# Packed key/value projection, input split moved into the last query tiles, last denominators summed apart from matmuls

## The reference

```
qkv = x @ Wqkv.T + b          # 16 query heads of 32, one key head and one value head of 32
P   = softmax(causal(q k.T / sqrt(32)));  ctx = P v;  a = ctx @ out_w.T + out_b
x1  = layernorm(x + a)        # no gain or bias
s   = x1 @ router_w.T         # 8 experts, the best 2, softmax of their 2 scores
y   = sum over the two experts of weight * (silu(x1 w1[e]) * (x1 w3[e])) w2[e]   # bf16
out = layernorm(x1 + y)
```

## Time and profile before

| | |
|---|---|
| time, median of 3 runs | 1130.98 us (1130.84 to 1131.72) |
| the profiled execution | 1128.94 us, span 1126.9 us |
| PE busy | 1083.4 us, 96% |
| DVE, ACT, POOL busy | 883.7, 718.4, 194.6 us |
| mean granted PE clock | 0.992 |
| scores L1170, values L1192 on PE | 327.3 and 286.7 us |
| exponentials L652 on ACT | 525.4 us |
| adds L829 on DVE | 403.4 and 64.0 us |

### The profile page before, as it was taken

One profiled execution on the slowest core, in us unless ns is written; L12 is line 12 of the kernel. 1 busy time (PEld: TensorE's weight loads), 2 busy tenths in 40 slices (PEclk: granted clock), 3 DMA queues, 4 the chain that ended last, 5 costly groups with the idle time before them and its releaser, 6 DMA issues.

```text
span 1126.9 us, 18411 instructions
## 1 busy us (share of the span) xinstructions
PE 1083.4 (96%) x6096; PEld 524.6 (47%) x6120; DVE 883.7 (78%) x1105; ACT 718.4 (64%) x852; POOL 194.6 (17%) x161
## 2 busy tenths in 40 slices
PE   8999999999999999999999999999999999999976
PEld 6365435643337433335634643474333654333442
DVE  4566899679976699987677679966998667898956
ACT  6744785478864498885445457644888437888821
POOL 3520332013110020111032013301211201211000
PEclk9899999999999999999999999999999999999999
DMA  4976401442001622001263253025400152200000
GB/s 141 210 115 145 119 1 39 103 122 39 1 2 47 141 76 38 1 1 40 64 143 98 58 130 75 3 59 130 113 1 1 39 122 67 39 1 2 1 2 38
DMA packets 40336, 72.31 MB, mean 64 GB/s; under 512 B 13968, under 2 KB 14992, under 8 KB 40208
## 3 DMA queue, kind: packets, MB, share of 16 engines
q1 hardware_dynamic: 24624, 56.64, 19.0%
q0 software_dynamic: 13584, 11.54, 7.0%
q10 hardware_dynamic: 2000, 2.51, 0.7%
HBM read 25.58 MB, written 8.39 MB: 30 GB/s over the span
## 4 chain that ended last, share of the span: by engine, by line
PE 80%; DVE 10%; issue 5%; POOL 2%; ACT 2%; DMA 1%; SPq 1%; DVEq 0%; ACTq 0%; POOLq 0%
PE sc L1170 21%; PE bank L1192 19%; PE sc L1032 10%; PE sc L1310 9%; PE bank L1032 7%; DVE psum_k L829 5%; PE sc L1210 3%; PE sc L1325 2%; PE bank L1210 2%; PE sc L1258 1%; POOL prob L517 1%; PE bank L1318 1%; DVE stats L905 1%; PE bank L1325 1%; DVE res L902 1%
## 5 line engine op out<-in xcount | busy, mean ns | idle before, releaser
L652 ACT ACTIVATE prob<-sc 128x1024 f32<-128x1024 f32 x544 | 525.4, 1025 | 130.8 <-PE sc L1170 130.7
L829 DVE TENSOR_TENSOR psum_k<-psum_k,prob 128x2048 f32<-128x2048 f32 x170 | 403.4, 2373 | 4.7
L1170 PE MATMUL sc<-q_st,k_st 128*128 128x512 f32 x1088 | 327.3, 423 | 9.4 <-DVE rden L878 3.8
L1170 PEld LDWEIGHTS sc<-q_st,k_st 128*128 128x128 f32 x1088 | 184.5, 189 | 250.6 <-ACT prob L652 177.3
L1192 PE MATMUL bank<-prob,v_sb 128*32 128x512 f32 x2176 | 286.7, 604 | 1.2 <-POOL prob L517 1.2
L517 POOL TENSOR_SCALAR_AFFINE_SELECT prob<-prob 128x1024 f32<-128x1024 f32 x64 | 113.2, 1817 | 530.7 <-ACT prob L652 530.7
L1310 PE MATMUL sc<-prob,w_sb 128*128 128x512 bf16 x488 | 116.9, 379 | 2.1 <-issue 1.3
L1192 PEld LDWEIGHTS bank<-prob,v_sb 128*32 128x32 f32 x2176 | 44.4, 108 | 105.5 <-issue 87.4
L682 ACT ACTIVATE prob<-sc 128x512 f32<-128x512 f32 x64 | 38.0, 594 | 73.0 <-PE sc L1310 72.7
L829 DVE TENSOR_TENSOR psum_k<-prob 128x2048 f32<-128x2048 f32 x28 | 64.0, 2287 | 20.7 <-POOL prob L517 16.2
L1032 PE MATMUL bank<-q_st,wq_hi 128*128 128x512 f32 x240 | 80.1, 398 | 0.0
(11 more groups left out here) (155 smaller groups left out, 1017.8 us busy)
## 6 DMA issues: line engine op xcount, KB each, us to landing
q_st<-q_hi SPq DMA_DIRECT2D x120, 128.0 KB, 2.4
q_st<-q_lo SPq DMA_DIRECT2D x120, 128.0 KB, 2.4
res<-in_x SPq DMA_DIRECT2D x8, 1024.0 KB, 5.2
res<-ob_sb POOLq DMA_DIRECT2D x8, 1024.0 KB, 8.6
out_x<-res SPq DMA_DIRECT2D x32, 256.0 KB, 2.0
res<-in_xT SPq DMA_DIRECT2D x7, 1024.0 KB, 4.9
w_sb<-in_w POOLq DMA_DIRECT2D x8, 256.0 KB, 8.6
prob<-in_wqkvT ACTq DMA_DIRECT2D x4, 288.0 KB, 6.3
```

Of the source, the lines that this page charges most:

```text
L652: nc.scalar.activation(prob[t % NP][:, half * HW:(half + 1) * HW], score_half(q // TB, 2 * t + half).rearrange("p m n -> p (m n)"), ACT.Ex ...
L829: nc.vector.tensor_tensor(acc[:, :], first[:, :], prob[t % NP][:, :], ALU.add).then_inc(add_v, 1)
L1170: last = nc.tensor.matmul(dst, k_st[:, k * P:(k + 1) * P], q_st[slot][:, c * HJ:(c + 1) * HJ, at:at + P], start=True, stop=not shift)
```

## The change

Four parts.

1. *Packed key/value projection.* The weights' high part and their low part stand side by side (128 columns), so one matmul with the input's high part gives both products, in partitions 0 to 63 and 64 to 127; a second one adds the input's low part to the first 64. That makes 8 matmuls. ACT then copies the first half with the bias to `kv_sum`, DVE adds the second half to it (`add_kv`), and ACT and DVE split k from `kv_sum` in SBUF.
2. *Packed norms.* `sum_squares` becomes 5 matmuls with constant weights of 32 columns: four write the sums of the query heads into the four partition quarters of one bank, the fifth adds those of k and v into one row. One maximum over 512 columns, one transpose, and one more small copy follow.
3. *Input split.* ACT makes `xT_hi` in four pieces behind the exponentials of the first four tiles of the block's last query tile, and POOL makes `xT_lo` in four.
4. *Order at the block's end.* The last query tile of each block leaves no tile to the matmuls with ones: DVE adds all. PE's order becomes output 0, next key/value, output 1, last denominators, output 2, next query 0, output 3, turning v, query 1, query 2. DVE adds residuals 0 and 1 before it normalises the last context. The split of the next query 0 now waits for output 3, as it overwrites the context.

```diff
-BY_PE = [0] + [1] * 9 + [2] * (NQ - 10)
+BY_PE = [0 if q == 0 or q % TB == TB - 1 else 1 if q < 10 else 2 for q in range(NQ)]
...
                         load_xT(g + 1)
-                        sp.wait_ge(xT_low, count(b, xT_low, g + 1))
+                        sp.wait_ge(xT_low, count(b, xT_low, DC * (g + 1)))
...
                     with if_more(pool, b, g):
-                        pool.wait_ge(xT_high, count(b, xT_high, g + 1))
-                        nc.gpsimd.tensor_tensor(out=xT_lo, in0=xT_raw[(g + 1) % 2],
-                                                in1=xT_hi.bitcast(F32), op=ALU.subtract).then_inc(xT_low, 1)
+                        for c in range(DC):
+                            pool.wait_ge(xT_high, count(b, xT_high, DC * g + c + 1))
+                            nc.gpsimd.tensor_tensor(out=xT_lo[:, c, :], in0=xT_raw[(g + 1) % 2][:, c, :],
+                                                    in1=xT_hi[:, c, :].bitcast(F32), op=ALU.subtract).then_inc(xT_low, 1)
...
             def split_high_k(b, g):
                 act.wait_ge(projected, count(b, projected, 5 * g + 1))
+                nc.scalar.activation(kv_sum, LOW[4][0:2 * HD, :], ACT.Identity, bias=bvk_sb[:, :]).then_inc(kv_half, 1)
+                act.wait_ge(kv_ready, count(b, kv_ready, g + 1))
                 cols = slice((g % NG) * BT, (g % NG + 1) * BT)
-                nc.scalar.activation(vT_sb[:, :], LOW[4][0:HD, :], ACT.Identity, bias=bvk_sb[0:HD, :])
                 for part in (0, 2):
-                    last = nc.scalar.activation(k_st[part * HD:(part + 1) * HD, cols], LOW[4][HD:2 * HD, :],
-                                                ACT.Identity, bias=bvk_sb[HD:2 * HD, :])
+                    last = nc.scalar.activation(k_st[part * HD:(part + 1) * HD, cols], kT_sb, ACT.Copy)
...
             def split_high_q(b, g, j):
+                if g and j == 0:
+                    act.wait_ge(outproj, count(b, outproj, TB * g))
                 act.wait_ge(projected, count(b, projected, 5 * g + 2 + j))
...
                         for n in range(TB - 1):
                             if split_at(TB * g + n, HIGH_LAG) == t:
                                 split_high_context(g, n)
+                        if FIRST[TB * g + TB - 1] <= t < FIRST[TB * g + TB - 1] + DC:
+                            with if_more(act, b, g):
+                                split_high_x(g + 1, t - FIRST[TB * g + TB - 1])
...
-                    with if_more(act, b, g):
-                        split_high_x(g + 1)
                     split_high_context(g, TB - 1)
...
+            def add_kv(b, g):
+                dve.wait_ge(kv_half, count(b, kv_half, g + 1))
+                dve.sem_inc(waited_apart, 1)
+                nc.vector.tensor_tensor(kv_sum, LOW[4][2 * HD:4 * HD, :], kv_sum, ALU.add).then_inc(kv_ready, 1)
...
+                nc.vector.reduce_max(norms[:, :], squares_bank(g)[:, :], AX).then_inc(norms_ready, 1)
...
+                def begin_residuals(g):
+                    dve.wait_ge(biased, count(b, biased, 16 * (g + 1)))
+                    for t in range(2):
+                        dve.wait_ge(outproj, count(b, outproj, TB * g + t + 1))
+                        residual(g, t, LOW[t], resid1)
...
                 def finish_attention(g):
-                    for t in range(TB):
+                    for t in range(2, TB):
                         if t == 3:
                             with if_more(dve, b, g):
-                                split_low_k(b, g + 1)
+                                add_kv(b, g + 1)
                         dve.wait_ge(outproj, count(b, outproj, TB * g + t + 1))
                         last = residual(g, t, LOW[t], resid1)
                     last.then_inc(mv_ready, 1)
                     with if_more(dve, b, g):
+                        split_low_k(b, g + 1)
                         split_low_q(b, g + 1, 0)
...
+                    begin_residuals(g)
                     normalise_context(TB * (g + 1) - 1)
...
+            def product_kv(c, high_rows=xT_hi, low_rows=xT_lo):
+                def high():
+                    return nc.tensor.matmul(LOW[4], wq_hi[:, c, D:D + 4 * HD], high_rows[:, c, :],
+                                            start=(c == 0), stop=(c == DC - 1))
+                if c == 0:
+                    high()
+                last = nc.tensor.matmul(LOW[4][0:2 * HD, :], wq_hi[:, c, D:D + 2 * HD], low_rows[:, c, :],
+                                        start=False, stop=False, skip_group_check=True)
+                return high() if c else last
...
+                rows = [squares_bank(g)[j * HD:(j + 1) * HD, :] for j in range(HJ)]
+                for j in range(HJ):
+                    nc.tensor.matmul(rows[j], head_pick[:, :], squares[:, j, :], start=True, stop=(j < HJ - 1))
+                last = nc.tensor.matmul(rows[HJ - 1], kv_pick[:, :], squares_kv, start=False, stop=True)
                 last.then_inc(normed, 1)
...
                 def finish_attention(g):
+                    with if_more(pe, b, g):
+                        project_kv(b, g + 1)
+                    project_out(g, 1)
                     denominators(TB * (g + 1) - 1)
-                    project_out(g, 1)
                     project_out(g, 2)
                     with if_more(pe, b, g):
-                        project_kv(b, g + 1)
+                        project_q(b, g + 1, 0)
                     project_out(g, 3)
                     with if_more(pe, b, g):
-                        project_q(b, g + 1, 0)
                         turn_v(b, g + 1)
```

More of the change, by code:

```diff
@@ L1054, in turn_v @@
             def turn_v(b, g):
[L1055 removed]
+                pe.wait_ge(kv_ready, count(b, kv_ready, g + 1))
                 pe.sem_inc(waited_apart, 1)
@@ L1104, in _ @@
                 pe.wait_ge(first_low, 2 * (c + 1))
[L1105 to L1108 removed]
+                last = product_kv(c, start_hi, start_lo)
+                if c == DC - 1:
+                    last.then_inc(projected, 1)
+                last = product(q_bank(0, 0), (wq_hi, wq_lo), (start_hi, start_lo), c, slice(0, P))
+            last.then_inc(projected, 1)
             for j in range(1, HJ):
```

84 lines of the change are left out of this document (33 added, 51 removed).

## The result

The changed kernel takes 1136.44 us, the median of 7 runs (1134.55 to 1137.85). Runs of the kernel before, taken beside them, have a median of 1130.98 us (1128.56 to 1131.79). The ratio is 1.0048 with a 95% interval of 1.0035 to 1.0061: slower by 0.5%, 5.5 us. That lies inside the predicted range of 1126 to 1139 us and inside the forecast's own 1128 to 1137, but 4.2 us above the point of 1132.2 us. It is also a slowdown, to which the prediction gave a chance of 0.37; the likeliest single outcome, with 0.40, was no change beyond 0.2%. The profiled execution took 1135.71 us, its span is 1134.0 us, and it is 6.8 us above that of before. The forecast was +1.2.

The account below looks back on a forecast made before the run. TensorE (PE), busy 96% of the span, was taken to bound the kernel. Gains and losses of 12 to 15 us summed to +1.2 us on the 1130.98 us median: 1132.2 us, range 1126 to 1139.

Parts of the forecast that it names:

- Packed projection and squares: Key/value projection saves 0.94 us in each of seven blocks (6.6 in all); norms and routing save 2.8 us.
- The start's 0.5: At the kernel's start the four spared key/value matmuls save only about 0.5 us, since DVE must deliver the last chunk.
- Cover of the last denominators: Block ends: PE's other work hides the denominators' chain before output 3, with 1 us to spare in block 3.
- Query 2's bank: Block ends: query 0's split waits for output 3, so PE waits 0.6 us (0 to 1.2) before query 2.
- The split inside the last tile row: POOL's pieces cost 0.9 us per met DVE add; PE waits 0.8 us in blocks 1 and 5.
- The port decides: Rival: every POOL piece delays DVE by its full length, 12 us slower, 1144 us; chance 0.12.
- Block 0: PE waits behind output 0 for POOL's subtraction, queued after expert loads; idle 7.6 us, then lower clock 2.3: +6.9 us.
- Block 4: ACT waits 2.1 us for the next input's transfer, and DVE's own last add costs 1.2: +2.0 us net.
- Block 7: No next projections cover the chain; PE idles 3.3 us before output 3, residual 3 +1.5, clock +0.5: +2.0 us.

Follow-up runs that it names:

- late_rows_alone: packed_only plus late last denominators behind output 1, last tile rows summed all on DVE, residuals 0 and 1 earlier; key/value projection not moved, input split whole: 1150.76 us.
- pieces_alone: packed_only plus the changed kernel's split of the next input in four pieces during the last tile row: 1132.41 us.
- filled_gap: Changed kernel with 22 unused transposes put on PE ahead of output 3 in the last block of the last sequence: 1134.95 us.
- residual_1_later: Changed kernel, but in each sequence's last block DVE takes residual 1 behind the last context and low context: 1132.76 us.
- packed_only: Kernel before plus only the packed key/value projection and packed norms; input split, orders and last denominators as before: 1126.14 us.
- mended: Changed kernel with the edits of kv_late_in_block_0 and filled_gap, plus query 0's low part made ahead of the keys' on DVE: 1121.50 us.
- kv_late_in_block_0: Changed kernel, but in each sequence's first block PE issues the next key/value projection behind output 2, not ahead of output 1: 1129.01 us.
- third_blocks_alone: packed_only plus input pieces and new end order in each sequence's third block alone, with query 0's low part ahead of the keys': 1120.95 us.
- loads_behind_pieces: Changed kernel, but POOL issues the first block's last two expert loads behind the four input pieces, not ahead: 1129.81 us.

## Why the prediction was right, and where not

**The forecast's shape held**: gains and losses of 12 to 15 us that nearly cancel, with block 0 the largest, and every wait that was foretold is in the trace. The likeliest outcome, no measurable change, did not come: the sum was +1.2 us and the time rose by 5.5 (6.8 in the profile). The time is in the range because most of the misses are small, not because large ones cancelled; but most of them are losses that were sized too low. No rival came true as a whole.

**Packed projection and squares (6.6 + 0.5 + 2.8).** The steps were right where they can be seen: 0.9 a projection, 0.2 to 0.6 a routing. But the parts measured together give 5.1 us, not 9.9. The start's 0.5 no run shows, and code waits (below) took 2 us in the profile. This is the term that was most over-sized: even the upper end of the interval (3.6 to 7.7) lies below it.

**Cover of the last denominators.** Right in blocks 2, 3 and 6: no wait ahead of them, no wait ahead of output 3. late_rows_alone shows what that cover is worth.

**Query 2's bank (0.6, bounds 0 and 1.2).** The trace of the changed kernel has 0.71 us in each of seven blocks, 5.0 in all; taking it away gave 6.4 us, 0.9 a block. The cause is as told, DVE's two subtractions for k ahead of the low part.

**The split inside the last tile row (0.9 for a piece that meets an add; 0.8 of wait in blocks 1 and 5).** Under-sized. An add that meets pieces took 1.0 to 1.1 us longer, and the two together 2.1, with no overlap to subtract; PE waited 1.30 us for the 0.8. Attention grew by 1.7 and 1.5 us in these blocks in pieces_alone and by 2.0 and 1.6 in the changed kernel, where 1.2 with ACT's share was forecast. The Trainium skill ("SBUF — State Buffer", "SBUF: two separate sides") has the shared port pair as an exclusive lock for the whole instruction. By this the price is a piece's own length: one of four takes 1.24 us where no DVE add stands beside it (4.94 / 4, block 0), and the trace's 1.0 to 1.1 lie closer to that than the 0.77 of masks did. "The port decides" didn't come true all the same: in blocks 2 and 3 the transposes were 0.7 and 0.6 us late, not 2.5, as the idle time of DVE takes up the rest.

**Block 0 (+6.9).** Right in mechanism and nearly in size: 8.0 us of wait for 7.6, half clock for nearly 4 us, 1.7 us lost to it where I took 2.3. The price of the clock came from a place that shows a price, but no fall behind a wait: in the trace of before the granted clock was 0.50 from 26 us on, with PE busy, 2 us ahead of the wait of 2.14 us that the earlier trace rows ends. Undoing the order gave 7.4, giving POOL another order 6.6.

**Block 4 (+2.0).** Under-sized by 1. The wait for the transfer was seen and taken too large (1.21 us for 2.1); the port was left out. Pieces met an add there too, and output 0 waited 1.49 us. In pieces_alone the attention of the block is 2.0 us longer for the split alone.

**Block 7 (+2.0, of which the clock 0.5 out of 0 to 2.8).** The wait was right (3.06 us for 3.3), and the clock was the mis-sized part: output 3 took 1.7 us longer. filled_gap and residual_1_later both remove that: with the wait filled, or at 1.41 us, output 3 ran at full clock, while in all five traces that have this wait at 3.0 to 3.1 us PE fell to the lower level within 2 us behind it. A further 1.9 us at the end of the profile is that half clock behind the last transposes, which other orders show too; it belongs to the execution.

Together, in the profile: block 7 and the end 2.7 us over the forecast, block 4 1.0, block 1 0.7, block 3 0.7, block 0 0.6, the others even. That is 5.7 us. The 1.9 at the end is scatter; of the rest the clock in block 7 and the port in blocks 1 and 4 are the parts that a run shows.

## What to carry to other kernels

Before work is moved ahead, ask on each queue what stands in front of what it needs: here two loads on POOL cost 7 us, an order of two subtractions on DVE 6, one residual 4, and each was mended by a line or two. A reorder that gains in long stages and loses in short ones can be made where it gains: with one line mended, the same edits take 5 us off packed_only when made in two blocks, and as they stood they add 10 when made everywhere. It is not the only way: made everywhere, but with its three losses mended one by one, it came to the same time (mended, 1121.50 us against 1120.95). And parts that lean on each other can't be priced alone: one of them, by itself, cost 25 us.

## What the runs showed of the hardware

**A wait of 2 to 3 us can bring the lower clock, and the same length need not.** At the end of block 0 PE stood at full clock behind waits of 1.96 us (kv_late_in_block_0), 2.45 (mended) and 2.59 (third_blocks_alone), and fell to 0.50 behind 1.95 us (late_rows_alone), 2.14 (loads_behind_pieces) and 2.60 (packed_only). So the length of the wait alone doesn't decide it in this stretch. Behind every wait of 3.0 us or more in these traces it fell. How long 0.50 lasted behind the 4.0 to 4.5 us of the last block was some 2.5 to 4 us in some traces and 8 or more in others. The Trainium skill ("TensorE: Matmul & The Clock Gate", "What's actually happening") says that the gate passes one of two rates, set by how busy PE has been of late; the trace agrees, with 1.00 and 0.50 in the windows and mixtures only where a change falls inside one.

**The first matmul behind a long branch body can stand still with no cause that the profile shows.** The first instruction of `finish_attention` on PE, behind the body of an `If`, waited 1.80 and 1.22 us in two blocks of before, 2.60 and 1.32 in packed_only, 2.59 in third_blocks_alone, 0.68 in one of the changed kernel, and not in most other blocks. The Trainium skill ("Runtime: NRT & Kernel Launch", "Instruction fetch mechanics") says that a taken branch whose target is not at hand forces a fetch before execution goes on. The places agree with it; no run here shows the fetch itself.
